# State-space stages of a two-layer block: sums over states as turns in PSUM, gate in [time, channel], part of u*B from TensorE

## The reference, cut to what matters

```
x, z = split(h @ in_proj)                # each [B, T, 512]
xc   = silu(causal_conv4(x) + conv_b)
dt, Bm, Cm = split(xc @ x_proj);  dt = softplus(dt @ dt_proj + dt_b)
h[t] = exp(dt[t] * A) * h[t-1] + (dt[t] * xc[t]) * Bm[t]    # per channel and state
y[t] = sum over states of h[t] * Cm[t];  y = (y + D * xc) * silu(z)
out  = y @ out_proj
```

## Time and profile before

| what | us |
|---|---|
| median of three runs | 2796.69 (2794.05 to 2799.36) |
| the profiled execution | 2800.64 |
| its span | 2798.8 |
| busy PE, DVE, ACT, POOL over the span | 2379.9, 2118.9, 1563.2, 1135.3 |

### The profile page before, as it was taken

How to read it: one execution, slowest core, us unless ns; L and a number is a source line. 1 busy time by engine, 2 the same in 40 slices (tenths; PEclk the granted TensorE clock), 3 DMA queues, 4 the chain that set the end, 5 groups by cost and what they waited for, 6 DMA issues and landing times.

```text
span 2798.8 us, 32693 instructions
## 1 busy us (share of the span) xinstructions
PE 2379.9 (85%) x11300; PEld 1600.5 (57%) x11300; DVE 2118.9 (76%) x3100; ACT 1563.2 (56%) x2734; POOL 1135.3 (41%) x829
## 2 busy tenths in 40 slices
PE   5989896689998798958995798897778987899998
PEld 2333432467776687847884234333333444799998
DVE  5999999699997365538894899999864653577776
ACT  6676574255665455516884866766313444266673
POOL 3889998200000444210221699989601134100004
PEclk9999999899999799979997899999867886799999
DMA  4032040570000000012421330303084231256553
GB/s 178 2 120 92 30 146 0 196 256 1 24 1 1 36 1 31 16 66 95 162 106 53 121 115 7 121 31 102 0 124 103 55 81 58 91 189 224 210 197 95
DMA packets 101607, 247.36 MB, mean 88 GB/s; under 512 B 9285, under 2 KB 65361, under 8 KB 94274
## 3 DMA queue, kind: packets, MB, share of 16 engines
q1 hardware_dynamic: 88530, 222.43, 24.6%
q0 software_dynamic: 5376, 14.70, 1.6%
q10 hardware_dynamic: 7536, 8.13, 1.2%
HBM read 187.96 MB, written 48.81 MB: 85 GB/s over the span
## 4 chain that ended last, share of the span: by engine, by line
PE 42%; DVE 25%; ACT 11%; issue 9%; POOL 9%; DMA 1%; SPq 1%; POOLq 1%; ACTq 1%; DVEq 0%
PE psum L111 7%; DVE psum L758 7%; PE psum L112 7%; PE psum L113 7%; PE psum L498 5%; POOL bu L372 4%; PE psum L118 3%; POOL ch L415 3%; ACT WH L3526 2%; ACT g L3673 2%; DVE ch L775 2%; PE psum L481 2%; DVE ch L758 2%; PE psum L2967 1%; PE psum L2895 1%
## 5 line engine op out<-in xcount | busy, mean ns | idle before, releaser
L372 POOL TENSOR_TENSOR bu<-u,row 128x1024 f32<-128x1024 f32 x254 | 594.8, 2354 | 137.0 <-DVE psum L758 47.5
L498 PE MATMUL psum<-ch,ident 128*128 128x512 f32 x1024 | 513.2, 634 | 114.6 <-DVE ch L775 63.7
L758 DVE TENSOR_TENSOR_SCAN psum<-psum,bu 128x1024 f32<-128x1024 f32 x210 | 479.8, 2285 | 22.1 <-ACT psum L590 21.2
L498 PEld LDWEIGHTS psum<-ch,ident 128*128 128x128 f32 x1024 | 190.4, 198 | 401.6 <-issue 184.1
L590 ACT ACTIVATE psum<-dt,A 128x511 f32<-128x511 f32 x512 | 332.1, 681 | 0.4
L775 DVE TENSOR_TENSOR ch<-psum,row 128x1024 f32<-128x1024 f32 x210 | 256.6, 1222 | 5.7
L3673 ACT ACTIVATE g<-psum,bias 128x256 f32<-128x256 f32 x248 | 101.1, 470 | 133.8 <-PE psum L113 129.6
L3495 POOL DMA_INDIRECT R<-m1res,gi x26 | 26.2, 1006 | 340.3 <-DMA m1res<-ob 324.2
L462 PE MATMUL psum<-hT,inw 128*128 128x512 f32 x256 | 130.0, 637 | 27.9 <-ACT xs L536 20.6
L111 PE MATMUL psum<-WH,hs 128*128 128x256 f32 x496 | 144.8, 292 | 5.0 <-DVE hs L3753 2.2
L111 PE MATMUL psum<-xT,WH 128*128 128x256 f32 x496 | 142.0, 286 | 7.6 <-DVE xT L3716 7.6
(11 more groups left out here) (456 smaller groups left out, 6536.7 us busy)
## 6 DMA issues: line engine op xcount, KB each, us to landing
W<-in_m1W SPq DMA_DIRECT2D x24, 2052.0 KB, 8.5
row<-Ascr SPq DMA_DIRECT2D x64, 512.0 KB, 5.7
row<-Bscr SPq DMA_DIRECT2D x64, 512.0 KB, 5.8
m1buf<-zt SPq DMA_DIRECT2D x8, 2048.0 KB, 17.0
W<-in_m0W SPq DMA_DIRECT2D x16, 1024.0 KB, 5.9
m1res<-ob ACTq DMA_DIRECT2D x23, 256.0 KB, 4.9
m0buf<-zt SPq DMA_DIRECT2D x2, 2064.0 KB, 18.0
xe<-m0buf SPq DMA_DIRECT2D x8, 516.0 KB, 8.0
```

The costliest lines, as they stand in the source:

```text
L372: e.tensor_tensor(m.bu[i % 3][:, :, :], u, m.row[:, g, 0, :, :], ALU.mult).then_inc(*m.fed.up)
L498: p = pe.matmul(m.y, k.ident, m.ch[i % RING_C][:, j, :], start=False, stop=g == UNITS - 1 and j == 1)
L758: dve.tensor_tensor_scan(to, flat, m.bu[i % 3][:, :, :].rearrange("p a n -> p (a n)"), 0.0, ALU.mult, ALU.add).then_inc(*m.scan.up)
```

## The change

Both Mamba stages change in the same way:
- The sum over states is done by turning matmuls: the 128 x 128 blocks of `ch` are stationary, the identity moves, and the results are accumulated in PSUM as [time, channel]: eight turns a unit instead of two 512-column products. D*xc is made by ACT (`m.dx`) and turned in as well (four turns a group).
- z is projected straight into [time, channel], the gate is done there (`m.yzT`), and the gated y is turned back by PE ("yt", four turns a group) and copied by ACT before "out".
- Units 3, 5 and 7 of each group (`FROM_PE`) get u*B from PE: u is turned ("ut", copied by ACT to `m.uT`) and multiplied by diagonal matrices of B (`m.diag_B`), eight 128 x 128 products a unit, written to the PSUM pair. DVE builds the diagonals, three operations a batch (`mamba_diag_dve`), from the turned B ("bt"). The decays of these units go to SBUF (`m.ad`, two buffers). `bu` has two buffers instead of three.
- The scans of units 2, 3, 5 and 7 write `ch`, and POOL does their C product; DVE does those of units 0, 1, 4 and 6.
- The convolution of the first channel block goes from POOL to PE. The slots of items, activations and statistics are new: z is made in the batch's own slots 1 to 4, and so on. The B rows of units 3, 5 and 7 are no longer transferred.

The diff, cut:

```diff
+FROM_PE = (3, 5, 7)
+BY_POOL = (2,)
...
+    m.uT, m.yzT, m.dx = al([128, 4, 128], "uT"), al([128, 4, 128], "yzT"), al([128, T], "dx")
...
+    m.diag_B = {g: m.row[:, g, 0, :, :].rearrange("p a (c t) -> p a c t", c=4) for g in FROM_PE}
+    m.bu = [al([128, 2, T], "bu") for _ in range(2)]
+    m.ad = [al([128, 2, T], "ad") for _ in range(2)]
...
-    m.y = k.psum[:, 6, :]
+    m.y = k.psum[:, 6, :].rearrange("p (c n) -> p c n", c=4)
...
-FIRST = [("h", 0), ("h", 1)] + [("in", i) for i in range(4)] + [("conv", 3), ("xp", 0)] + [("dt", i) for i in range(4)]
-OPENING = {0: ("z", 0), 1: ("z", 1), 2: ("z", 2), 3: ("z", 3)}
-BEFORE = {2: ("out", 0), 3: ("out", 1), 4: ("out", 2), 5: ("out", 3)}
-AHEAD = {6: ("h", 0), 7: ("h", 1), 8: ("in", 0), 9: ("in", 1), 11: ("in", 2), 12: ("in", 3),
-         14: ("conv", 1), 16: ("conv", 2), 18: ("conv", 3),
-         21: ("xp", 0), 22: ("dt", 0), 23: ("dt", 1), 24: ("dt", 2), 25: ("dt", 3),
-         26: ("z", 0), 28: ("z", 1), 29: ("z", 2), 30: ("z", 3)}
+FIRST = [("h", 0), ("h", 1)] + [("in", i) for i in range(4)] + [("conv", 3), ("xp", 0)] + [("dt", i) for i in range(4)] + [("bt", 0)]
+FIRST_BANKS = (0, 1, 2, 3, 4, 5, 6, 7, 0, 1, 3, 6, 2)
+OWN = {1: ("z", 0), 2: ("z", 1), 3: ("z", 2), 4: ("z", 3), 13: ("yt", 0), 18: ("yt", 1), 25: ("yt", 2)}
+BEFORE = {1: ("yt", 3), 6: ("out", 0), 8: ("out", 1), 10: ("out", 2), 12: ("out", 3)}
+AHEAD = {5: ("h", 0), 6: ("h", 1), 7: ("in", 0), 9: ("in", 1), 11: ("in", 2), 14: ("in", 3),
+         15: ("conv", 0), 17: ("conv", 1), 19: ("conv", 2), 21: ("conv", 3),
+         23: ("xp", 0), 24: ("dt", 0), 25: ("dt", 1), 26: ("dt", 2), 27: ("dt", 3), 30: ("bt", 0)}
...
+    if i == 0:
+        o.append(("ut", 0, 0))
     if b and s in BEFORE:
         o.append((BEFORE[s][0], b - 1, BEFORE[s][1]))
+    if s in OWN:
+        o.append((OWN[s][0], b, OWN[s][1]))
+    if s % UNITS == 6 and i // UNITS + 1 < 4 * B:
+        n = i // UNITS + 1
+        o.append(("ut", n // 4, n % 4))
...
-    return n % UNITS in (2, 5) and (b == B - 1 or n in (2, 5, 18, 21, 26))
+    return from_pe(i) or i % UNITS in BY_POOL
...
-            for j in range(2):
+            for j in (1,) if g in FROM_PE else range(2):
...
-        e.wait_ge(*m.fed(UNITS * (s - 2) + UNITS - 1))
+        e.wait_ge(*m.fed(NTH[UNITS * (s - 2) + 6]))
+        e.wait_ge(*m.full(mamba_use("ut", (s - 2) // 4, (s - 2) % 4)))
...
-    if i >= 3:
-        e.wait_ge(*m.scan(i - 3))
+    if n >= 2:
+        e.wait_ge(*m.scan(FED[n - 2]))
...
+def mamba_input_pe(k, m, pe, i):
+    s, g = i // UNITS, i % UNITS
+    b, db = s // 4, s % 4
+    if g == FROM_PE[0]:
+        pe.wait_ge(*m.drawn(mamba_use("ut", b, db)))
+    if db == 0:
+        n = FROM_PE.index(g)
+        pe.wait_ge(*(m.diag_in(2 * b + n) if n < 2 else m.drawn(mamba_use("bt", b, 0))))
+    if i >= RING_A:
+        pe.wait_ge(*mamba_left(m, i - RING_A))
+    for j in range(2):
+        for c in range(4):
+            p = pe.matmul(m.a[i % RING_A][:, j, 128 * c:128 * c + 128], m.uT[:, c, :], m.diag_B[g][:, j, c, :], start=True, stop=True)
+    p.then_inc(*m.fed_pe.up)
...
+    if from_pe(i) and i // UNITS % 4 == 0:
+        pool.wait_ge(*m.rows[i % UNITS](i // PER))
...
-        if i + 2 < PER * B:
+        if i + 2 < PER * B and not from_pe(i + 2):
...
-        if b + 1 < B and 9 <= n < 16:
-            mamba_conv_pool(k, m, pool, b + 1, n - 9)
         if i in (1, 2, 3):
             if i == 1:
                 pool.wait_ge(*m.soft(3))
             mamba_dt(k, m, pool, i)
-        if 28 <= n and b + 1 < B:
-            if n == 28:
+        if n == 0 and b:
+            mamba_dt(k, m, pool, 4 * b + 3)
+        if 29 <= n and b + 1 < B:
+            if n == 29:
                 pool.wait_ge(*m.soft(3 * b + 6))
-            mamba_dt(k, m, pool, 4 * (b + 1) + n - 28)
-        if n % UNITS == 4 and i // UNITS + 1 < 4 * B:
+            mamba_dt(k, m, pool, 4 * (b + 1) + n - 29)
+        if n in (4, 12, 20) or n == 29 and b + 1 < B:
...
+    elif w == "z":
+        for f in range(2):
+            p = pe.matmul(bank, m.hT[:, f, 128 * j:128 * j + 128], m.inw[:, f, T:2 * T], start=f == 0, stop=f == 1)
+    elif w == "ut":
+        s = 4 * b + j
+        pe.wait_ge(*m.u_in(s))
+        for c in range(4):
+            p = turn_in(k, pe, bank[:, 128 * c:128 * c + 128], m.u[s % 2][:, 128 * c:128 * c + 128])
+    elif w == "yt":
+        pe.wait_ge(*m.gated(4 * b + j))
+        for c in range(4):
+            p = turn_in(k, pe, bank[:, 128 * c:128 * c + 128], m.yzT[:, c, :])
+    elif w == "bt":
+        pe.wait_ge(*m.drawn(mamba_use("xp", b, 0)))
+        W = R + 32
+        for c in range(4):
+            p = turn_in(k, pe, bank[:, W * c:W * c + W], m.xd[0:W, 128 * c:128 * c + 128])
...
+        if i + 2 < PER * B and from_pe(i + 2):
+            mamba_input_pe(k, m, pe, i + 2)
         if g == 0:
-            pe.wait_ge(*(m.gated(s - 1) if s else m.diag(1)))
-            pe.matmul(m.y, m.dg[:, 12 + s % 4, :], m.xc[:, s % SIX, :], start=True, stop=False).then_inc(*m.direct.up)
+            if s:
+                pe.wait_ge(*m.gated(s - 1))
+            pe.wait_ge(*m.dx_in(s))
+            for c in range(4):
+                p = pe.matmul(m.y[:, c, :], m.dx[:, 128 * c:128 * c + 128], k.ident, start=c == 0, stop=False, is_transpose=True)
+            p.then_inc(*m.direct.up)
         pe.wait_ge(*mamba_out(m, i))
         for j in range(2):
-            p = pe.matmul(m.y, k.ident, m.ch[i % RING_C][:, j, :], start=False, stop=g == UNITS - 1 and j == 1)
+            for c in range(4):
+                p = pe.matmul(m.y[:, c, :], m.ch[i % RING_C][:, j, 128 * c:128 * c + 128], k.ident, start=False,
+                              stop=g == UNITS - 1 and j == 1 and c == 3, is_transpose=True)
         p.then_inc(*m.summed.up)
+    mamba_item_pe(k, m, pe, "yt", B - 1, 3)
...
+    elif w == "ut":
+        act.copy(m.uT[:, :, :], bank.rearrange("p (c n) -> p c n", c=4)).then_inc(*m.drawn.up)
+    elif w == "yt":
+        act.copy(m.yz[:, j, :], bank).then_inc(*m.drawn.up)
     else:
-        if s >= SIX:
-            act.wait_ge(*m.gated(s - SIX))
-        act.copy(m.sz[:, s % SIX, :], bank).then_inc(*m.drawn.up)
...
+    act.activation(m.sz[:, :, :], m.sz[:, :, :], ACT.Silu).then_inc(*m.sz_in.up)
+def mamba_direct_act(k, m, act, s):
+    act.wait_ge(*m.xc_in(s))
+    if s:
+        act.wait_ge(*m.direct(s - 1))
+    act.activation(m.dx[:, :], m.xc[:, s % SIX, :], ACT.Identity, scale=pv(k, m.L + "D", 4)[:, s % 4:s % 4 + 1]).then_inc(*m.dx_in.up)
...
+    if from_pe(i):
+        e = NTH[i]
+        if e >= 2:
+            act.wait_ge(*m.scan(FED_PE[e - 2]))
+        else:
+            act.wait_ge(*m.zeros(2))
+        a = m.ad[e % 2]
+    else:
+        if i >= RING_A:
+            act.wait_ge(*mamba_left(m, i - RING_A))
+        a = m.a[i % RING_A]
+        act.copy(a[:, :, 0], m.zero[:, :])
...
+        if i in (8, 9):
+            for j in range(8) if i == 8 else range(4):
+                o, n0 = (m.dg, 4) if i == 8 else (m.dg0, 0)
+                g = act.activation(o[:, j, :], k.ident, ACT.Identity, scale=cw[:, n0 + j:n0 + j + 1])
+            g.then_inc(*m.diag.up)
+        if n == 14 and b:
             x_stats_act(k, act, 4 * (m.rnd + 1) + b - 1)
-        if n == (2 if b else 4):
+        if n == 5:
             mamba_gate_act(k, m, act, b)
-        if n == 5 and b + 1 < B:
+        if n == 4 and b + 1 < B:
             mamba_rows_act(k, m, act, b + 1)
-        if n == 19 and b + 1 < B:
+        if n % UNITS == 3 and i // UNITS + 1 < 4 * B:
+            mamba_direct_act(k, m, act, i // UNITS + 1)
+        if n == 22 and b + 1 < B:
             mamba_silu_act(k, m, act, b + 1)
-        if n in (24, 25) and b + 1 < B:
-            mamba_soft_exp_act(k, m, act, b + 1, 2 * (n - 24), 2 * (n - 24) + 2)
-        if n == 26 and b + 1 < B:
+        if n in (26, 27) and b + 1 < B:
+            mamba_soft_exp_act(k, m, act, b + 1, 2 * (n - 26), 2 * (n - 26) + 2)
...
+    if s:
+        dve.wait_ge(*m.full(mamba_use("yt", (s - 1) // 4, (s - 1) % 4)))
+    dve.tensor_tensor(m.yzT[:, :, :], m.y, m.sz[:, :, 128 * db:128 * db + 128], ALU.mult).then_inc(*m.gated.up)
...
+def mamba_diag_dve(k, m, dve, b, n):
+    u = mamba_use("bt", b, 0)
+    W, g = m.R + 32, FROM_PE[n]
+    if n == 0:
+        dve.wait_ge(*m.full(u))
+    elif n == 2:
+        dve.wait_ge(*m.drawn(u - 1))
+    rows = mamba_bank(k, m, u)[:, 0:4 * W].rearrange("p (c w) -> p w c", c=4)[:, m.R + 2 * g:m.R + 2 * g + 2, :]
+    dve.tensor_tensor(m.diag_B[g], k.ident.unsqueeze(1).unsqueeze(1).to_broadcast([128, 2, 4, 128]),
+                      rows.unsqueeze(3).to_broadcast([128, 2, 4, 128]), ALU.mult).then_inc(*(m.diag_in.up if n < 2 else m.drawn.up))
...
+        if from_pe(i):
+            dve.wait_ge(*m.fed_pe(NTH[i]))
+            decays, inputs = m.ad[NTH[i] % 2][:, :, :], a
+        else:
+            dve.wait_ge(*m.fed(NTH[i]))
+            decays, inputs = a, m.bu[NTH[i] % 2][:, :, :]
```

(41 more changed lines are left out.)

96 lines of the change are left out of this document (38 added, 58 removed).

## The result

The changed kernel takes 2939.1 us (median; 2934.2 to 2944.7) against 2795.9 for the kernel before in the same measurement: a ratio of 1.0511 (1.049 to 1.0533), 143 us slower. The forecast was 2877, with 2760 to 2940 as the range over all cases and 2835 to 2925 as the forecast's own. The side held. The wide range held by 0.9 us, the forecast's own was missed, and the size was little more than half of what came (81 against 143 us). Both Mamba stages carry it: the last gate of stage A is at 576.71 us instead of 509.61 (+67.1), the stage's last addition of the output at 588.54 instead of 517.56 (+71.0), the last gate of stage B at 2156.88 instead of 2018.54 (+138.3), and the span grew by 138.0. Batches are counted 0 to 3 from here on; A to D are the four groups of a batch.

What follows compares the result with a forecast made beforehand. The loop through POOL and PE was taken as the bound, queue order deciding. Per stage 27.4 + 12 + 3.3 = 42.7, taken as 40; both stages +80 on 2800.6 gave 2880.6, median 2877; range 2760 to 2940, own 2835 to 2925.

Steps and rivals of the forecast that it cites:

- The side: Whole kernel: forecast slower than before, chance 0.68, against faster 0.28 and same 0.04.
- The loop: Gate end to gate end: VectorE scans, POOL's meets and inputs, PE's turns of unit 7, gate; 26.4 us if nothing intervenes.
- Prices and loads: PE 0.118 us a turn, 0.12 a product record; loads per batch VectorE 103, POOL 94.5, ACT 82, PE 102 us.
- Rival 4: PE's u*B products cost 0.43 us a record, PE 162 us a batch, time 3149; chance 0.11 together with the clock rival.
- Group C: Third group of a batch: xp waits for ACT's silu, itself behind the copy of turned u; gate at 33.5 us.
- Group A: First group of a batch: ACT's long run delays the copy of u, h1, in0 and turns of unit 7; 33 us.
- The sum: Per Mamba stage: middle batches +13.7 each, first +12, last and end +3.3; 42.7, taken as 40 us.
- the signs: Gates 30 us or more apart in the first three batches; VectorE's busy share in the stages down to about 80%.
- the meets in POOL's loop: C products on POOL (meets 2, 3, 5, 7), queued among inputs and u; POOL's part of the loop 17.6 us.
- the order of slot items before u*B on PE: Slot-3 items precede unit 5's u*B, costing their length less 0.65 us; slot-7 items precede the turns that release the gate.
- Rival 1: Faster: PE's items fit into slack and POOL's loop decides; 109.1 us a batch, 2761 us in all; chance 0.28.
- Rival 3: Slower still: PE at half clock in half of 32 groups adds 80, about 2957 us; chance 0.11 together with Rival 4.

Runs made afterwards that it cites:

- e6: Changed kernel, but in slot 22 ACT does the silus of xc ahead of the copy of the turned u: 1.0397 to the kernel before.
- e1: Changed kernel, but PE issues u*B of unit i+2 ahead of the items of slot i: 1.0532 to the kernel before.
- e2: Changed kernel, but the items of slots 3 and 7 of each group come behind that unit's sum on PE: 1.0571 to the kernel before.
- e11: Changed kernel, but POOL does only the C products of units 2 and 5, DVE those of 3 and 7 too: 1.0431 to the kernel before.
- e5: Changed kernel, but u*B all on POOL, no diagonals or turned u, three bu buffers, C products shared as before; new slots stay: 1.0122 to the kernel before.
- e4: Changed kernel, but the C product of unit 7 is done by DVE, not POOL: 1.0394 to the kernel before.
- e7: Changed kernel with unit 7's C product on DVE, gate's silu in slot 6, silus of xc ahead of the copy of turned u: 1.0342 to kernel before.
- e10: Changed kernel with unit 7's C product on DVE, gate's silu in slot 6, preparation one slot earlier from conv1 on: 1.0463 to the kernel before.
- e9: Changed kernel with u*B all on POOL, preparation one slot earlier from conv1 on, gate's silu in slot 6: 1.0092 to the kernel before.
- e12: Changed kernel with u*B all on POOL and preparation in the old kernel's slots, except statistics, left in slot 14: 1.0155 to the kernel before.

## Why the prediction was right, and where it was short

**The loop.** The last batch has little but the loop in it. Forecast 26.4 a group at the full level; measured 28.0, 27.1 and 25.4 (the last without the next group's inputs). Forecast +2 for that batch, measured 113.8 against 110.9, +2.9. This step held, also that DVE idles before every gate: 1 to 8.6 us in stage A.

**Prices and loads.** 0.118 a turn, measured 0.109 (eight in 0.87 us); 0.12 a product record, 0.111. Rival 4 is out. The Trainium skill (TensorE: Matmul & The Clock Gate, Part 4: PE-mode transpose) puts a turn at about 275 ns in a kernel, beside a figure for bf16. The trace agrees for the duration of one in f32 (273 ns, median), but turns in a row start 0.109 us apart, and that is what counts here. The loads of a batch were near: DVE 103 forecast and 100.1 measured in batch 1, POOL 94.5 and 93.7, ACT 82 and 82.7. PE's sum of 102 came to 110.6. It had also put the kernel before at 97, where the earlier trace rows shows 104.1, so the step up was read better (+5, measured +8.2) than the level.

**Group C.** The step named was xp waiting for silu, silu for the copy of u, the copy for PE behind u*B of unit 7. The chain after, batch 1 (start us, us, what):

```profile
270.70 3.43 PE psum L506 x8
274.13 1.78 PE psum L405 x16
...
277.67 3.44 PE psum L506 x8
281.10 1.78 PE psum L405 x16
...
284.23 0.59 ACT uT L587
...
284.84 1.28 ACT L621
...
286.67 1.66 ACT xc L621 x3
...
288.47 3.60 PE psum L510 x8
292.07 1.04 PE psum L543 x8
```

From 269.61 to 284.21 the chain stays on PE, then ACT copies and runs silu, then xp. 33.5 forecast, 33.5 here. In batches 0 and 2 C takes 36.5 and 35.2, 3.0 and 1.7 us more, and that is xp at the half level: 6.61 and 5.30 us instead of 3.60, after the same 3.4 us without work. That batch 1 hit the forecast is in that respect luck: in all six groups C of the two stages xp was at the full level twice. e6 confirms the step by undoing it.

**Group A.** The step was right, its size wrong: 33 forecast, 37.85 measured. The chain:

```profile
205.42 1.79 PE psum L482 x4
207.21 1.78 PE psum L405 x16
...
212.10 2.08 ACT xn L759 x4
...
216.00 1.28 ACT L626
...
217.29 1.91 ACT sz L626
...
219.27 1.28 ACT L656
...
221.86 0.52 ACT uT L587
...
222.43 1.12 PE psum L118 x4
223.54 1.71 PE psum L543 x8
225.25 3.37 PE psum L479 x4
228.62 0.89 PE psum L543 x8
```

The order is the forecast's: z2, u*B, z3 and its copy, then row activations, silu between two table loads, decays, the copy of u, h1, turns of unit 6, in0, turns of unit 7. PE holds the chain from 198.19 to 211.60, ACT from then to 222.38. The turns of unit 7, forecast at 31 to 33 us after the gate's end (192.3), began at 36.3. One part of that is in0: it takes 3.37 us instead of 1.72, and the eight turns of unit 6 take 1.71 instead of 0.87, after PE had waited for ACT: the half level stands inside the path and makes 2.5 us of the 4.9 missing. The rest is not taken apart. The four groups' stretches show the level:

```profile
192.00:229.50 37.50, 31.62 (x161) 23.07 (x162) 24.67 (x15) 20.29 (x35) 24.51 (x12) 0.83 0.01 4
229.50:259.60 30.10, 28.09 (x168) 21.69 (x167) 25.99 (x24) 16.81 (x31) 22.07 (x10) 1.00 0.01 1
259.60:293.10 33.50, 28.38 (x157) 19.10 (x157) 23.40 (x14) 20.18 (x36) 22.49 (x11) 1.00 0.00 1
293.10:325.90 32.80, 22.55 (x136) 16.95 (x136) 25.73 (x16) 25.47 (x41) 24.34 (x13) 0.82 0.61 205
```

PEclk (third number from the end) is 0.83 in A and 0.82 in D, where PE waits for ACT and POOL, and 1.00 in B and C. I had counted the half level for the last batch only. D came to 32.7 and 34.1 against 31.5 for the same reason. The eight turns after meet 7 took 1.98 us, twice the 1.0 at the full level, and in batch 2 the u*B of a unit in its chain took 3.73 instead of 1.78.

**The sum.** Forecast a stage: middle batches +13.7 each, first +12, last and end +3.3, 42.7, cut to 40. Measured +19.9 and +22.2 (137.06 against 114.88, from the gates in both traces), +22.1, +2.9: 67.1 up to the last gate. Behind it came 3.9 where 1.3 was forecast (the output projection took 9.19 us instead of 7.17 after another wait for ACT), so 71.0 a stage. The terms that were too small are A, the half level in A and D and in xp of C (I had put it at nothing outside the last batch), the first batch (+12 against +22.1), the end, and the rounding from 42.7 to 40 for delays that one group was to absorb from the other: none did. Of the signs, gates 30 us apart or more in the first three batches held but for one (28.9, stage B), and DVE's share fell to 75%, not 80%. That 2939 lies inside 2760 to 2940, by 0.9 us, owes something to luck: the forecast's own range ended at 2925.

**The cause by parts.** I put the cost on two places: the meets in POOL's loop and the order of slot items before u*B on PE. Both exist, but e1 and e2 show that order alone is no remedy, and e11 and e5 give shares: turns with gate and slots 1.2 points, u*B on PE 3.1, meets 0.8 (1.2 by e4, which takes only meet 7 off POOL). They are differences between variants that differ in more than one thing. With the feed e5 also drops the diagonals and the turn and copy of u, has a third `bu` buffer, and gives POOL five meets a batch in batches 0 to 2, where e11 has eight. POOL's inputs waited 24.0 us of batch 1 for scans after the change and 6.2 before; no run has the feed with three buffers, so that rival is not excluded.

By group, from e11 to e5 in batch 1: A 37.45 to 32.45, B 30.10 to 30.43, C 35.18 to 28.71, D 32.01 to 29.75. So the feed costs nothing in B, where PE is fullest (28.1 of 30.1 us busy), and most in A and C, where a long run of PE's queue ends in a wait for ACT and PE's next item is often at the half level. The copy of u ahead of silu and the level of xp are shown by e6, 1.1 points. The rest of the 3.1 is argued from the chains above, not isolated.

Rival 1 (faster, POOL's loop decides) assumed that PE's items fit into slack; the variants with the slack rearranged stayed at 1.034 (e7) and 1.046 (e10). Rival 3 (the clock) is part of the truth: 0.90 against 0.99 in the middle batches. Whether turns keep the clock up is not settled: it was 1.00 in group B with 64 sum turns among dense items, and low only in stretches that also had gaps. So the rule of the Trainium skill that the prediction names (TensorE: Matmul & The Clock Gate, Part 4: PE-mode transpose) is neither confirmed nor refuted here.

No variant beats the kernel before; the best is e9 at 1.0092.

## What to carry to other kernels

Engine sums below the present period say nothing when one queue must serve several deadlines in order: write out, from one fixed event to the next, what stands in the queues between them, and believe the sum. When a delay moves with every reordering, take work off the queue (here u*B back to POOL) rather than shuffle it. Look for the places where one engine's long run ends in a wait for another: moving one activation ahead of one copy gave 1.1 points here. A cheaper matmul on PE can lengthen its gaps, and the price at the half level is paid by the next item. When a variant is to put an old order back, compare every slot of it with the old kernel: in e12 the statistics were left behind, and the run decides nothing.

## What the runs showed of the hardware that was not expected

- A turn and a 128-column f32 product record cost the same in a run at the full level: 0.109 us (eight in 0.87) and 0.111 us (sixteen in 1.78). The product needs two records and the turn one.
- The granted clock was 1.00 in group B of batch 1, where 64 turns, 48 product records and dense items kept PE busy 28.1 of 30.1 us, and 0.83 in group A at 31.6 of 37.5 us, its longest gap 2.3 us, for ACT.
- The same gap does not cost the same. After 3.4 us without work the eight records of xp took 3.60, 5.30 or 6.61 us in three batches of one run.
